# One decoder layer on one core: the last feed-forward stage's element-wise work dealt out anew over VectorE, ScalarE and GpSimd

## The reference

```python
def act_quant(x):
    scale = 127.0 / jnp.clip(jnp.max(jnp.abs(x), axis=-1, keepdims=True), 1e-05)
    return jnp.clip(jnp.round(x * scale), -128, 127) / scale

h = bit_linear(x, w1)                                   # 512 -> 2048
h = depthwise_conv1d(h.transpose(0, 2, 1), conv_w, conv_b)   # three taps along the tokens, plus a bias
h = h.transpose(0, 2, 1)
h = jax.nn.silu(h)
return bit_linear(h, w2)                                # 2048 -> 512
```

## Time and profile before

| | |
|---|---|
| median of the three runs | 3478.45 us |
| the profiled execution | 3476.95 us, of which its span 3475.4 us |
| PE busy | 3150.0 us, 91% |
| DVE busy | 2338.6 us, 67% |
| ACT busy | 1766.6 us, 51% |
| POOL busy | 1176.7 us, 34% |
| cross FFN, PE's first to last w1/w2 product | 2280.1 to 3007.7 us |
| last FFN, from the first `dequantise` to the end | 3040.1 to 3475.4 us |

### The profile page before, as it was taken

The page is one execution under the profiler, slowest core; times in us unless marked ns, Lnnn a source line. Parts: engine busy times, 40 slices in busy tenths (PEclk is TensorE's granted clock), DMA queues, the critical chain, the costliest instruction groups (busy, mean ns, idle before and its releaser), DMA issues. The chain is left out here.

```text
span 3475.4 us, 57137 instructions
## 1 busy us (share of the span) xinstructions
PE 3150.0 (91%) x19234; PEld 2284.4 (66%) x19234; DVE 2338.6 (67%) x4193; ACT 1766.6 (51%) x3130; POOL 1176.7 (34%) x909
## 2 busy tenths in 40 slices
PE   6999899999999999979998788879999999768886
PEld 5777566666666666657776677668888888534443
DVE  5562788888888888745644588835555444589996
ACT  3331788888888888712222322232222222176662
POOL 3343411231123112244442355521111111068886
PEclk9999899999999999989999899989999999899999
DMA  6774321222122212265552644431111110300112
GB/s 215 248 238 165 98 64 58 76 77 63 58 75 76 62 57 76 76 213 210 197 202 111 183 130 123 142 111 41 41 43 42 41 43 31 110 25 31 62 49 67
DMA packets 239351, 350.53 MB, mean 101 GB/s; under 512 B 31792, under 2 KB 129104, under 8 KB 239184
## 3 DMA queue, kind: packets, MB, share of 16 engines
q1 hardware_dynamic: 208256, 290.41, 25.9%
q0 software_dynamic: 8912, 32.82, 2.9%
q10 hardware_dynamic: 22016, 25.17, 2.0%
HBM read 210.68 MB, written 137.64 MB: 100 GB/s over the span
## 5 line engine op out<-in xcount | busy, mean ns | idle before, releaser
L887 DVE CUSTOM_DVE_ANT_0 attend_scores<-attend_scores,attend_bias_table 128x1024 f32<-128x1024 f32 x512 | 630.4, 1231 | 164.5 <-PE attend_scores L741 161.2
L814 ACT ACTIVATE attend_probs<-attend_scores,attend_neg_max 128x1024 f32<-128x1024 f32 x512 | 571.3, 1116 | 141.1 <-DVE attend_neg_max L887 131.0
L753 PE MATMUL attend_turned<-ident,attend_probs 128*128 128x128 f32 x4096 | 557.4, 275 | 12.6 <-DVE attend_probsT L895 12.5
L753 PEld LDWEIGHTS attend_turned<-ident,attend_probs 128*128 128x128 f32 x4096 | 473.2, 141 | 120.9 <-DVE attend_probsT L895 29.8
L741 PE MATMUL attend_scores<-attend_k_stack,attend_q_stack 96*128 96x512 f32 x1024 | 373.7, 447 | 17.8 <-DMA attend_q_stack<-qk_parts 14.7
L822 ACT COPY attend_probsT<-attend_turned 128x512 f32<-128x512 f32 x640 | 359.1, 583 | 24.7 <-PE attend_turned L753 23.1
L2235 DVE TENSOR_TENSOR cross_ffn_h_lo<-cross_ffn_hidden,cross_ffn_h_hi 128x512 fp32r<-128x512 f32 x128 | 96.0, 755 | 363.9 <-ACT cross_ffn_h_hi L2126 363.2
L703 POOL TENSOR_TENSOR attend_out_parts<-attend_out_full,attend_out_parts 128x256 fp32r<-128x256 f32 x64 | 46.5, 726 | 847.1 <-ACT attend_out_parts L829 847.1
L768 PE MATMUL attend_out_acc<-attend_probsT,attend_v_in 128*32 128x256 f32 x4096 | 312.9, 390 | 0.7 <-DVE attend_out_full L905 0.7
L741 PEld LDWEIGHTS attend_scores<-attend_k_stack,attend_q_stack 96*128 96x128 f32 x1024 | 154.4, 190 | 174.7 <-issue 157.3
L895 DVE COPY attend_probsT<-attend_turned 128x512 f32<-128x512 f32 x384 | 263.5, 686 | 1.3 <-PE attend_turned L753 1.3
(11 more groups left out here) (291 smaller groups left out, 6650.0 us busy)
## 6 DMA issues: line engine op xcount, KB each, us to landing
qk_parts<-qkv_qk_out SPq DMA_DIRECT2D x64, 512.0 KB, 3.2
attend_k_stack<-qk_parts SPq DMA_DIRECT2D x192, 128.0 KB, 2.5
attend_q_stack<-qk_parts SPq DMA_DIRECT2D x192, 128.0 KB, 2.7
qkv_wq_raw<-L_ffn_w POOLq DMA_DIRECT2D x16, 1024.0 KB, 7.6
o_parts<-attend_out_parts ACTq DMA_DIRECT2D x64, 256.0 KB, 2.5
carried_o_in<-o_parts SPq DMA_DIRECT2D x32, 512.0 KB, 6.2
qkv_x_in<-x SPq DMA_DIRECT2D x8, 1024.0 KB, 5.9
v_rows<-qkv_v_out SPq DMA_DIRECT2D x32, 256.0 KB, 3.4
```

Source lines behind the costliest of these rows:

```text
L753: last = pe.transpose(turned[:, x, c], probs[:, i % 2, k * P:(k + 1) * P], ident[:, :])
L814: act.activation(probs[:, i % 2], scores[:, i % 2], ACT.Exp, bias=neg_max[:, i % 4:i % 4 + 1], scale=-1.0, accum_out=den[:, qg % 2, j, h:h ...
L887: dve.tensor_tensor_reduce(scores[:, i % 2], scores[:, i % 2], bias_table[:, h, at:at + T], -1.0, BIG, ALU.add, ALU.min, neg_max[:, i % 4: ...
```

## The change

Nothing of the result is changed; work is moved between engines, and queues are reordered.

- The right tap is no longer made by ACT and added by POOL. DVE does both outer taps: `add_left` now writes back into the PSUM tile `centre`, and a new `add_right` reads `centre` and `y` and writes `conv`. `right_tap` is gone. `find_max` of another block stands between the two. `y` has three buffers.
- Rounding is on ACT, by two activations with a constant column as bias (`round_up` in place on `h_scaled`, then `round_down` into `hqT`), with SiLU of another block between them. In the last unit it stays on DVE (`round_last`).
- `finish` is split: ACT scales `out_acc` into `out` (`scale_out`), POOL adds `x2_in` (`add_x`). PE's next product waits for `out_scaled`. In the last unit it stays one DVE instruction (`finish_last`). PE's last product waits for `out_scaled` as well.
- POOL sets the border column (`set_edge`) and writes `diag` (`set_diag`).
- All lags from SiLU on are one step shorter.
- The copy of the identity stands at the end of `load_vectors`.

```diff
@@ cross_ffn
                 pool.dma_start(tile[:, :], row(vector, 0, D)).then_inc(rows_loaded, 16)
+            pool.tensor_copy(ident16[:, :], ident[:, :]).then_inc(ident16_ready, 1)
 
         def gpsimd(pool):
-            pool.tensor_copy(ident16[:, :], ident[:, :]).then_inc(ident16_ready, 1)
             pool.wait_ge(rows_loaded, 4 * 16)
@@ quantised_ffn
-    SILU_AT, TURN_AT, MAX_AT = 3, 4, 5
-    SPREAD_AT, SCALE_AT, ROUND_AT = HB + 5, HB + 6, HB + 7
+    TAPS_AT, SILU_AT, TURN_AT, MAX_AT = 2, 2, 3, 4
+    SPREAD_AT, SCALE_AT, ROUND_AT = HB + 4, HB + 5, HB + 6
@@ gpsimd
+            def set_diag(u):
+                pool.wait_ge(scale_step, (u + 1) * SCALE_STEPS)
+                past(pool, spread_ready, u)
+                pool.tensor_tensor(diag[:, :, :], ident[:, :].unsqueeze(1).to_broadcast([P, HT, P]),
+                                   h_scale[:, :].unsqueeze(2).to_broadcast([P, HT, P]), ALU.mult).then_inc(diag_ready, 1)
+
+            def add_x(j):
+                pool.wait_ge(x2_loaded[j % 4], (j // 4 + 1) * 16)
+                pool.wait_ge(out_scaled, j + 1)
+                pool.tensor_tensor(out[:, j % 2], out[:, j % 2], x2_in[:, j % 4], ALU.add).then_inc(out_done, 1)
...
             for s in range(END):
+                if s < SLOTS:
+                    set_edge(s)
+                u = half_at(s, SPREAD_AT)
+                if u is not None:
+                    set_diag(u)
                 i = block_at(s, SCALE_AT)
                 if i is not None:
                     scale_block(i)
-                i = block_at(s, 1)
-                if i is not None:
-                    add_right(i)
-
+                j = finish_at(s)
+                if j is not None:
+                    add_x(j)
@@ tensor
-            for t in range(2):
-                past(pe, out_done, (LAST - 1) * HT + t + 3)
+            pe.wait_ge(out_scaled, LAST * HT)
@@ scalar
+            def round_up(i):
+                act.wait_ge(h_scaled_ready, i + 1)
+                act.activation(h_scaled[:, i % 2], h_scaled[:, i % 2], ACT.Identity, bias=round_up_col[:, :]).then_inc(h_raised, 1)
+
+            def scale_out(j):
+                u, t = divmod(j, HT)
+                act.wait_ge(out_ready, j + 1)
+                past(act, stored[j % 2], j // 2 * 16)
+                act.activation(out[:, j % 2], out_acc[:, j % 2], ACT.Identity, scale=h_unit[:, u % 3, t:t + 1]).then_inc(out_scaled, 1)
...
             for s in range(END):
                 if s < SLOTS:
-                    set_edge(s)
                     taps_of(s)
+                j = finish_at(s)
+                if j is not None:
+                    scale_out(j)
+                r = block_at(s, ROUND_AT)
+                if r is not None and r < LAST * HB:
+                    round_up(r)
                 i = block_at(s, SILU_AT)
                 if i is not None:
                     silu(i)
+                if r is not None and r < LAST * HB:
+                    round_down(r)
@@ vector
+                dve.scalar_tensor_tensor(out=centre[:, i % 2], in0=y[:, u % 2, i % YR, 0:HALF], scalar=taps[:, f, 0:1], in1=centre[:, i % 2],
+                                         op0=ALU.mult, op1=ALU.add).then_inc(left_added, 1)
+
+            def add_right(i):
+                u, f = divmod(i, HB)
+                dve.wait_ge(left_added, i + 1)
                 past(dve, silu_done, i - CR + 1)
+                dve.scalar_tensor_tensor(out=conv[:, i % CR], in0=y[:, u % 2, i % YR, 2:HALF + 2], scalar=taps[:, f, 2:3], in1=centre[:, i % 2],
+                                         op0=ALU.mult, op1=ALU.add).then_inc(right_added, 1)
...
             for s in range(END):
+                c = block_at(s, TAPS_AT)
+                if c is not None:
+                    add_left(c)
                 i = block_at(s, MAX_AT)
                 if i is not None:
                     find_max(i)
+                if c is not None:
+                    add_right(c)
                 if s < SLOTS:
                     dequantise(s)
```

103 lines of the change are left out of this document (48 added, 55 removed).

## The result

| | before | after |
|---|---|---|
| median of the runs | 3478.78 us (3474.91 to 3482.97, 4 runs) | 3435.07 us (3433.70 to 3439.49, 4 runs) |
| ratio to before | | 0.9876, 95% interval 0.9859 to 0.9893 |
| span of the profiled execution | 3475.4 us | 3432.8 us |

The account below looks back on a forecast made before the run. VectorE and GpSimd were taken to be tied to each other at 2.65 us a slot in the last FFN. The terms 17.2 - 3 + 15 + 2.5 + 5.4 = 37.1 us gave 3441.4 us from 3478.45; range 3425 to 3461.

Parts of the forecast that it names:

- step C: Last FFN, the other six units: ScalarE holds slots at 2.61 us, 273.4 against 288.8 us; gain 15 us.
- the signs that I named: Trace after: ScalarE fullest, over 0.9; GpSimd near 0.75; taps 0.73; PE's cross FFN wait about 5.5 us, ended by L1787.
- A: Start of the cross FFN: with the identity copied earlier, PE starts at 2262.9 in place of 2280.1; gain 17.2 us.
- The term "0" for the start of the cross FFN: Cross FFN from PE's first product to the first dequantise: no change in length, 1 to 3 us if cover is thinner.
- B: Last FFN, first two units: VectorE's slot goes from 2.24 to 2.52 us with both outer taps; loss 3 us.
- D: Last FFN, from the last block to the last spread: 14.9 us becomes 12.4; gain 2.5 us.
- E: Tail, S being the last spread: the last finishes begin at S + 35.2 instead of S + 40.6; gain 5.4 us.
- 1 (C about 0): Last FFN: queues are tighter than busy times say, the slot stays at 2.70 us; 3456 us; chance 0.15.
- 2 (ScalarE isn't the bound, 3432, with C at 24): Last FFN: VectorE at 2.52 us a slot and boundaries hidden; gain there 24 us, 3432 us; chance 0.10.
- 3 (the tail keeps its length): Tail: three additions lie between GpSimd's last products, so no gain there; 3447 us; chance 0.08.
- 4 (A is 9): Cross FFN start: VectorE's normalisation until 2270.7 holds PE, gain there only 9 us; 3449 us; chance 0.06.
- 5 (PSUM in place is dear): VectorE's outer taps in every slot: in-place PSUM work costs more, 3488 us at 0.45 extra a slot; chance 0.03.

Follow-up runs that it names:

- Experiment 3: The kernel after with the left tap's sum written to SBUF instead of back to PSUM, right tap added there: 3454.62 us, 19.6 slower than after.
- e8: The run of Experiment 3, left tap's sum to SBUF in the kernel after: 3454.62 us, ratio to before 0.9933.
- e3: The kernel after with ScalarE's upward rounding step left out in units 0 to 6: 3420.13 us, 14.9 less than after.
- e7: The kernel after with four output tiles and four store counts in place of two: 3433.57 us, 1.5 less than after.
- e9: e7 plus the last unit's x2 loads issued right behind the stores of the tiles they replace: 3429.89 us, 5.2 less than after.
- e6: The kernel after with the output of units 0 to 6 finished by one VectorE instruction, replacing scale_out and add_x: 3442.90 us, 7.8 slower than after.
- e5: The kernel after without GpSimd's last four pairs of normalisations (gamma and beta of mix_out's last four tiles): 3436.63 us in a single execution.

## Why the prediction was right, and where it wasn't

**What bounds the kernel.** VectorE and GpSimd tied to each other: the earlier trace rows show it, and the gain came. (The first of the two instructions that the text calls GpSimd's additions is a product; the 2.65 stands.) Experiment 3 ties them again by one operand, and 17.4 of step C's 22.8 us are gone. That is a tie of the same kind, not the same one; no run took work off one of the two in the kernel before. Of the signs that I named, one failed: the fullest engine is VectorE (42.5 of 43.8 us), not ScalarE (42.0), and GpSimd is at 0.65, not near 0.75. PE's wait is ended 1.3 us behind the 2263 that I gave, but by the instruction that I named.

**A.** The step is right to 0.1 us (PE starts at L1787's end, 17.2 gained), and its cover was thinner than I took it. I wrote that VectorE's first part of the hidden layer isn't wanted before 2271 and that a thinner cover costs 1 to 3 us. The first part was in time. The second wasn't, and for a reason that the text named for the last FFN only: two engines with two SBUF inputs each. The term "0" for the start of the cross FFN should have been 2.5.

**B.** -3.5 against -3. The taps took 0.65 or 0.66 start to start, with 744 and 735 ns; the upper bound of +0.08 wasn't needed.

**C.** 22.8 against 15, the largest miss. Three sizes make it up. First, 2.6: I subtracted the forecast for 96 slots from a window that holds 95 intervals. Second, 0.4 that I rounded off "for waits that I can't see". Third, 5.0 over the six units (270.8 forecast for 95 intervals, 265.8 measured): a plain unit is 43.9, not 44.7, one with borders 46.4 to 47.6, not 47.9. I let ScalarE hold all 16 slots at 2.61. It holds only the four with a `scale_out`, and part of what it owes there it makes up in VectorE's slots; the mean, (12 x 2.51 + 4 x 2.84) / 16 = 2.59, came out near mine, and by chance. The slots make 0.3 of the 0.8 us of a plain unit; the other 0.5 is the boundary, where scales, spread and `scale_row` cost 2.4 us over the slots and I had 2.9. Of the two units with borders, the longer one has a slot of 3.84 us at a granted clock of 0.59, and the other 2.62 at 1.00. The prices were good: roundings 0.61 start to start, `scale_out` 0.57 (I took 0.61), `diag` on GpSimd 1.04 (I took 1.2 to 1.5).

**The tie between VectorE and GpSimd.** I wrote that if the rule on two SBUF inputs failed, GpSimd's operations would take 1.46 and the sum would stand. That looked at the wrong engine: GpSimd has room, VectorE hasn't. In e8 the lock-out costs VectorE 0.3 to 0.9 us in 31 slots, and the kernel 19.6 us; of GpSimd's operations only `add_x` grows, 1.30 to 1.49.

**D.** 3.2 against 2.5; no experiment was aimed at it. In e3, with one rounding less on ScalarE, it is 1.3 shorter still (10.4 in place of 11.7 us), so ScalarE's queue is in that chain, as the step said.

**E.** 6.6 against 5.4, and by the chain that was written down: `scale_out` of tile 27 waits for a store and starts at S + 18.3 (done by 19.2 forecast, 19.0 measured), then 64 products of 15.0 us (15.4). What the step didn't see is how many limits lay together: with the store chain gone, x2's loads hold the end 1.0 us sooner (e7), and with those gone GpSimd's queue does another 3.0 sooner (e9).

**The rivals.** 1 (C about 0) is out: the slot fell. 2 (ScalarE isn't the bound, 3432, with C at 24) is nearer to the measured time and to the measured C than the forecast. Its slot of 2.52 holds for 10 of 16; that ScalarE doesn't bind is refuted by e3's 14.9 us, and its hidden boundaries by the 2.4 us above. So the time can't tell the two apart; the slots do, and they stand between them. 3 (the tail keeps its length) is out, and e6 shows what would have made it true. 4 (A is 9) is out by the row at 2264.32. 5 (PSUM in place is dear) is out: 744 against 735 ns, where its threshold was some 0.9 us; the price is on the other route.

**The total.** It is nearer than its parts. C, D and E were 9.7 us too small together; the start of the cross FFN (2.5), a later end of the stage ahead of it (1.4; it differs from run to run by more than that) and B (0.5) took 4.4 of that back.

## What to carry to other kernels

When two engines meet at the same pace, look at their operands before their work: a VectorE instruction with two SBUF inputs beside a busy GpSimd can last until GpSimd's run ends (6.87 us for 2.28 in e5, 1.62 for 0.74 in e8), and one input in PSUM avoided it here. When a step is balanced, one relief tells you little about the next: 15 and 14 us alone, 48 together. And behind a wait that you remove, list each transfer in the same queue, not only the next engine: this tail had three limits within 4 us.
